# Seven half-block products in place of eight in the third sweep of a symmetric-storage graph kernel

## The reference, cut to what matters

```
h = relu(layernorm(x));  T1 = adj @ h;  T2 = 2 * adj @ T1 - h;  T3 = 2 * adj @ T2 - T1
x = x + (h @ W0 + T1 @ W1 + T2 @ W2 + T3 @ W3 + bias0)
h2 = relu(layernorm(x));  p = tanh(min(|h2|, 10)) * h2 / (|h2| + 1e-8)
s = adj @ p;  y = artanh(min(|s|, 0.999)) * s / (|s| + 1e-8)
x = x + (y @ K + bias1)
```

## Time and profile before

| | |
|---|---|
| median of 3 runs | 1854.3 us |
| the profiled execution | 1854.24 us, span 1852.4 us |
| TensorE busy | 1830.2 us, 99% of the span |
| VectorE, ScalarE, GpSimd busy | 413.7, 121.3 and 41.1 us |
| loads of blocks | 626 of 1 MB, 357 GB/s over the span |
| third sweep | about 1141 us to the end |

### The profile page before, as it was taken

How to read it: one execution, slowest core, us unless ns; L and a number is a source line. 1 busy time by engine, 2 the same in 40 slices (tenths; PEclk the granted TensorE clock), 3 DMA queues, 4 the chain that set the end, 5 groups by cost and what they waited for, 6 DMA issues and landing times.

```text
span 1852.4 us, 22385 instructions
## 1 busy us (share of the span) xinstructions
PE 1830.2 (99%) x9620; PEld 825.3 (45%) x9620; DVE 413.7 (22%) x853; ACT 121.3 (7%) x233; POOL 41.1 (2%) x65
## 2 busy tenths in 40 slices
PE   7999999999999999999999999999999999999997
PEld 4444444444444445444444444344444444444444
DVE  7111111111122123000000001532321222122136
ACT  1000000000000000000000000311000000000014
POOL 0000000000000000000000000000000000000003
PEclk9999999999999999999999999999999999999998
DMA  9999999999999986888888785899999999999995
GB/s 379 421 421 421 421 420 416 387 394 389 399 371 381 374 331 228 319 295 298 295 302 304 263 303 208 331 379 377 372 383 395 384 377 382 407 384 384 406 397 202
DMA packets 94833, 662.31 MB, mean 358 GB/s; under 512 B 11408, under 2 KB 13712, under 8 KB 14608
## 3 DMA queue, kind: packets, MB, share of 16 engines
q1 hardware_dynamic: 93744, 660.64, 91.5%
q10 hardware_dynamic: 992, 0.23, 0.1%
HBM read 658.74 MB, written 2.10 MB: 357 GB/s over the span
## 4 chain that ended last, share of the span: by engine, by line
PE 97%; DVE 1%; DMA 1%; SPq 0%; issue 0%; ACT 0%; DVEq 0%
PE row_bank L523 36%; PE work_bank L503 19%; PE work_bank L537 17%; PE row_bank L492 12%; PE row_bank L525 4%; PE own_bank L553 3%; PE work_bank L505 3%; PE turned L608 2%; DMA ring<-adj_blocks 1%; PE work_bank L577 0%; SPq L417 0%; PE own_bank L564 0%; PE own_bank L608 0%; PE row_bank L608 0%; SPq L428 0%
## 5 line engine op out<-in xcount | busy, mean ns | idle before, releaser
L525 PE MATMUL row_bank<-ring,nodes 128*64 128x512 f32 x1728 | 756.6, 592 | 0.0
L523 PE MATMUL row_bank<-ring,nodes 128*64 128x512 f32 x1728 | 756.6, 592 | 0.0
L523 PEld LDWEIGHTS row_bank<-ring,nodes 128*64 128x64 f32 x1728 | 236.4, 137 | 419.0 <-issue 416.2
L505 PE MATMUL work_bank<-ring,nodes 128*64 128x512 f32 x936 | 420.8, 592 | 0.0
L503 PE MATMUL work_bank<-ring,nodes 128*64 128x512 f32 x936 | 420.8, 592 | 0.0
L537 PE MATMUL work_bank<-ring,nodes 128*64 128x512 f32 x1456 | 342.2, 592 | 0.3 <-DVE nodes L888 0.2
L492 PE MATMUL row_bank<-ring,nodes 128*64 128x512 f32 x1112 | 269.8, 596 | 6.2 <-DMA ring<-adj_blocks 6.2
L525 PEld LDWEIGHTS row_bank<-ring,nodes 128*64 128x64 f32 x1728 | 236.4, 137 | 0.0
L503 PEld LDWEIGHTS work_bank<-ring,nodes 128*64 128x64 f32 x936 | 127.9, 137 | 218.8 <-issue 218.8
L537 PEld LDWEIGHTS work_bank<-ring,nodes 128*64 128x64 f32 x1456 | 124.4, 137 | 169.6 <-issue 167.8
L784 DVE TENSOR_TENSOR partial<-partial,work_bank 128x512 f32<-128x512 f32 x148 | 101.7, 688 | 332.5 <-PE work_bank L537 331.4
(11 more groups left out here) (106 smaller groups left out, 518.4 us busy)
## 6 DMA issues: line engine op xcount, KB each, us to landing
ring<-adj_blocks SPq DMA_DIRECT2D x626, 1024.0 KB, 7.7
out<-resid SPq DMA_DIRECT2D x16, 128.0 KB, 1.9
resid<-x SPq DMA_DIRECT2D x7, 256.0 KB, 11.4
resid<-x SPq DMA_DIRECT2D x2, 128.0 KB, 3.5
w_raw<-cheb_weight ACTq DMA_DIRECT2D x2, 64.0 KB, 7.8
bias<-cheb_bias ACTq DMA_DIRECT2D x1, 32.0 KB, 2.8
bias<-hyp_bias ACTq DMA_DIRECT2D x1, 32.0 KB, 3.8
w_raw<-hyp_kernel ACTq DMA_DIRECT2D x2, 16.0 KB, 8.8
```

What stands on the lines that cost most here:

```text
L505: done = nc.tensor.matmul(bank[EVEN, :], nodes[:, c * C + k, B, :], data[:, k, :], start=k == 0, stop=k == C - 1)
L523: nc.tensor.matmul(bank[ODD, :], nodes[:, c * C + k, A, :], data[:, k, :], start=first and k == 0, stop=last and k == C - 1)
L525: done = nc.tensor.matmul(bank[EVEN, :], nodes[:, c * C + k, B, :], data[:, k, :], start=first and k == 0, stop=last and k == C - 1)
```

## The change

For the `BOTH` visits of rows 6 to 15 in the third sweep (95 visits), a block is cut in four: contraction chunks 0-1 and 2-3, columns 0-255 (`N1`) and 256-511 (`N2`); the 64 features are cut in two halves of 32 (`H`). The product of these 2 by 2 halves is made with seven products in place of eight (the form of Strassen and Winograd). Each product is 2 chunks by 2 levels of 32 features by 256 columns, so a visit is 28 products (56 instructions) in place of 8 products of 64 by 512 (16 instructions). They lie in four column tiles of 32, at partitions 0, 32, 64 and 96. The partial products add up in both row banks, which one row now uses together.

- VectorE makes the three sums of the block's parts, 128 by 1024, 128 by 512 and 128 by 512, into one of two mix slots, in the program two visits ahead of the visit that uses them. TensorE waits for them ahead of its second, fourth and sixth group of products.
- GpSimd makes four sums of the features of a column, 128 by 128 each, after `EXPAND` (`SUMS`), for columns 0 to 13.
- At a row's end ScalarE copies one half bank and exchanges the 32-partition parts of another bank (5 copies), and VectorE makes the row from the four quarters (`JOIN`, six instructions), two visits after the row; its `TURN` is five visits after the row in place of two. The first fast visit of the next row waits until the banks are read.
- Two ring slots become mix slots and four hold the feature sums, so that from row 4 to the last `BOTH` visit the ring of blocks has 7 slots in place of 13.
- `OWN` and level-4 `AGAIN` visits, and `TURN`s of levels 3 and 4, also use 32-column tiles: twice as many products of half the width (16 in place of 8 for a `TURN`).
- `weight_terms()` makes a small mask that is used in `JOIN`.

```diff
+MIX_SLOTS, SUM_SLOTS = (7, 8), (9, 10, 11, 12)
+FAST_FROM = 6
...
+        if level == 3 and row >= FAST_FROM:
+            follow(2 if row < NB - 1 else 1, ("JOIN", row), lambda: None)
+            visits_to_turn = 5
...
+        if last > shared_from:
+            for k in MIX_SLOTS + SUM_SLOTS:
+                slot_free[k] = max(slot_free[k], shared_to)
...
+                if i in mix_no:
+                    n, mixed = mix_no[i], ring[:, MIX_SLOTS[mix_no[i] % 2], :, :]
...
+                    rounds = [(("A11", "B11", 0, high, N1), ("A11", "B11", 1, high, N1)),
+                              (("A12", "B21", 0, low, N1), ("S3", "T3", 0, low, N2)),
+                              (("A12", "B21", 1, low, N1), ("S3", "T3", 1, low, N2)),
+                              (("S4", "B22", 0, low, N2), ("S2", "T2", 0, high, N2)),
+                              (("S4", "B22", 1, low, N2), ("S2", "T2", 1, high, N2)),
+                              (("S1", "T1", 0, high, N2), ("A22", "T4", 0, low, N1)),
+                              (("S1", "T1", 1, high, N2), ("A22", "T4", 1, low, N1))]
+                    for k, pair in enumerate(rounds):
+                        if k in (1, 3, 5):
+                            pe.wait_ge(s_mixed, 3 * n + (k + 1) // 2)
+                        for part, (a, b, h, bank, columns) in enumerate(pair):
+                            for level in (A, B):
+                                lane = level * F + part * H
+                                done = nc.tensor.matmul(bank[lane:lane + H, columns], left(a, h, level), right[b][:, h, :],
+                                                        start=first and k < 2, stop=k == 6, tile_position=(0, lane),
+                                                        skip_group_check=True)
...
-                        for half in (0, 1):
-                            part = slice(half * F, (half + 1) * F)
+                        for lane in range(0, P, size):
+                            part = slice(lane, lane + size)
...
+                for j in mix_before.get(i, []):
+                    n = mix_no[j]
+                    dve.wait_ge(s_visit, visit_no[fast[n - 2]] if n >= 2 else shared_from)
+                    dve.wait_ge(s_landed[slot_of[load_of[j]]], uses_of[load_of[j]] * 16)
+                    nc.vector.tensor_tensor(mixed[:, :, N1].rearrange("p (k h) n -> p k h n", k=2), halves[:, :, :, N2],
+                                            block[:, 0:2, :].rearrange("p h (k n) -> p k h n", k=2), ALU.subtract)\
+                        .then_inc(s_mixed, 1)
+                    dve.wait_ge(s_mixed, 3 * n + 1)
+                    nc.vector.tensor_tensor(mixed[:, 0:2, N2], block[:, 2:4, N2], mixed[:, 0:2, N1], ALU.subtract)\
+                        .then_inc(s_mixed, 1)
+                    dve.wait_ge(s_mixed, 3 * n + 2)
+                    nc.vector.tensor_tensor(mixed[:, 2:4, N2], block[:, 2:4, N1], mixed[:, 0:2, N2], ALU.subtract)\
+                        .then_inc(s_mixed, 1)
```

More of the change, by code:

```diff
@@ L86, in next_is_known @@
         if kind == "AGAIN":
-            return (level[0], col) in known and (level[0] < 4 or ("SUM", row, 3) in steps)
+            summed = ("JOIN", row) if row >= FAST_FROM else ("SUM", row, 3)
+            return (level[0], col) in known and (level[0] < 4 or summed in steps)
         return (2 + sweep[0], col) in known
@@ L159, in work_order, with with_sums @@
         one_visit_passed()
-    return with_batches(steps)
+    return with_batches(with_sums(steps))
+def with_sums(steps):
+    out, waiting, corner = [], [], True
+    for s in steps:
+        out.append(s)
+        if s[0] == "EXPAND" and s[1] < NB - 2:
+            waiting.append(("SUMS", s[1]))
+        if s == ("AGAIN", LOW, LOW, 4):
+            corner = False
+        if not corner:
+            out += waiting
+            waiting.clear()
+    return out
 def is_loaded(kind, row, col, level=0):
@@ L245, in chebyshev_hyperbolic_kernel @@
             turn_no[s[1:]] = turns
+    fast = [i for i, s in enumerate(steps) if s[0] == "BOTH" and phase_of[i] == 2 and s[1] >= FAST_FROM]
+    mix_no = {i: n for n, i in enumerate(fast)}
+    in_order = [i for i, s in enumerate(steps) if s[0] in VISITS]
+    mix_before = {}
+    for i in fast:
+        mix_before.setdefault(in_order[in_order.index(i) - 2], []).append(i)
+    sums_no = {s[1]: n + 1 for n, s in enumerate(s for s in steps if s[0] == "SUMS")}
+    shared_from, shared_to = visit_no[steps.index(("AGAIN", LOW, LOW, 4))], visit_no[fast[-1]]
     slot_free = [0] * SLOTS
     for n, last in enumerate(last_visit_of):
+        if last > shared_from:
+            for k in MIX_SLOTS + SUM_SLOTS:
+                slot_free[k] = max(slot_free[k], shared_to)
         slot = min(range(SLOTS), key=lambda k: slot_free[k])
@@ L316, in chebyshev_hyperbolic_kernel @@
             known_at[s[1], 4] = n
+    fast_rows = [s[1] for s in steps if s[0] == "SUM" and s[2] == 3 and s[1] >= FAST_FROM]
+    for i in fast:
+        assert freed_by[load_of[i]] < visit_no[in_order[in_order.index(i) - 2]]
     norm_at = {s[1]: n + 1 for n, s in enumerate(s for s in steps if s[0] == "NORM")}
@@ L411, in chunks, with features, sum_of @@
             return slice(r * C, (r + 1) * C)
+        H = F // 2
+        N1, N2 = slice(0, BLOCK // 2), slice(BLOCK // 2, BLOCK)
+        def features(c, half, chunk_half):
+            return nodes[:, c * C + 2 * chunk_half:c * C + 2 * chunk_half + 2, :, half * H:(half + 1) * H]
+        feature_sums = ring[:, SUM_SLOTS[0]:SUM_SLOTS[-1] + 1, :, :].rearrange("p s k n -> p (s k) n")
+        def sum_of(c, k):
+            return feature_sums[:, c, k * 4 * H:(k + 1) * 4 * H].rearrange("p (h l f) -> p h l f", h=2, l=2)
         @block.sync
@@ L510, in _ @@
+                if kind == "BOTH" and phase_of[i] > 0 and i not in mix_no:
                     level = phase_of[i] + 1
@@ L534, in _ @@
                     pe.wait_ge(s_landed[slot], landed)
[L535 to L538, removed]
+                    if level < 4:
+                        for k in range(C):
+                            half = (ODD, EVEN)[k % 2]
+                            done = nc.tensor.matmul(bank[half, :], nodes[:, c * C + k, A if level == 3 else B, :],
+                                                    data[:, k, :], start=k < 2, stop=k >= 2)
+                    else:
+                        for k in range(C):
+                            for part in range(2):
+                                lane = k % 2 * F + part * H
+                                done = nc.tensor.matmul(bank[lane:lane + H, :],
+                                                        nodes[:, c * C + k, B, part * H:(part + 1) * H], data[:, k, :],
+                                                        start=k < 2, stop=k >= 2, tile_position=(0, lane))
                     done.then_inc(s_visit, 1)
@@ L551, in _ @@
                     for k in range(C):
-                        half = (ODD, EVEN)[k % 2]
-                        done = nc.tensor.matmul(bank[half, :], nodes[:, c * C + k, A, :], data[:, k, :],
-                                                start=first and k < 2, stop=last and k >= 2)
+                        for part in range(2):
+                            lane = k % 2 * F + part * H
+                            done = nc.tensor.matmul(bank[lane:lane + H, :],
+                                                    nodes[:, c * C + k, A, part * H:(part + 1) * H], data[:, k, :],
+                                                    start=first and k < 2, stop=last and k >= 2, tile_position=(0, lane))
                     done.then_inc(s_visit, 1)
@@ L659, in _ @@
                         .then_inc(s_high, 1)
-                if kind == "SUM" and s[2] == 3 and s[1] > LOW:
+                if kind == "SUM" and s[2] == 3 and s[1] in fast_rows:
+                    r = s[1]
+                    if r > FAST_FROM:
+                        act.wait_ge(s_cleared, fast_rows.index(r))
+                    else:
+                        act.wait_ge(s_visit, visit_no[steps.index(("H_TERM", NB - 1))])
+                    act.wait_ge(s_visit, visit_no[last_of_row["ROW", r, 3]])
+                    nc.scalar.activation(common[:, 1, :], row_banks[1][:, N2], ACT.Copy).then_inc(s_aside, 1)
+                    for lane in range(0, P, F):
+                        for to, come in ((0, H), (H, 0)):
+                            nc.scalar.activation(aside[lane + to:lane + to + H, :], row_banks[1][lane + come:lane + come + H, :],
+                                                 ACT.Copy).then_inc(s_aside, 1)
+                elif kind == "JOIN":
+                    r = s[1]
+                    act.wait_ge(s_joined, fast_rows.index(r) + 1)
+                    nc.scalar.activation(partial[EVEN, r, :], joined[EVEN, :], ACT.Copy).then_inc(s_kept, 1)
+                elif kind == "SUM" and s[2] == 3 and s[1] > LOW:
                     r = s[1]
```

81 lines of the change are left out of this document (76 added, 5 removed).

## The result

The changed kernel takes 1893.1 us (median of 4 runs, 1891.3 to 1896.3) against 1854.2 us before (1853.6 to 1854.9): ratio 1.0212, 95% interval 1.0194 to 1.0229. It is 39 us slower; 1836 was forecast, range 1814 to 1870.

The account below looks back on a forecast made before the run. TensorE was taken as the bound, with DMA 6 to 9% behind. Terms -40.7 + 1 + 7.4 + 0.8 + 4 + 8 + 2 = -17.5, with overlap -18.3, took 1854.3 to 1836 us; range 1814 to 1870.

Parts of the forecast that it names:

- The fast visits: Third sweep, rows 6 to 15: each of 95 `BOTH` visits takes 3.00 us in place of 3.43, -40.7 us.
- rival C: Four tiles don't run abreast, or issue is slower than 28.7 ns: 1900 us to over 2300; chance 0.09.
- The `TURN`s: Levels 3 and 4, 32 instructions for 16: +7.4 us (0 to 7.4) at level 3, +0.8 at level 4.
- Switches of width: Rows 4 and 5, some six changes between 64-wide and 32-wide visits, 0.17 us each: +1 us (0 to 1).
- VectorE's and GpSimd's sums: VectorE's three per block take 1.22, 0.69, 0.69 us, GpSimd's under 3 us per column: +4 us (0 to 20).
- Rival B: VectorE becomes the bound, its sums slowed by DMA and TensorE using the same memory: 1855 us or slower; chance 0.05.
- `JOIN` and the tail: `JOIN` at row ends hidden, also after row 15: 0; loads of columns 14 and 15: +2 us (0 to 6).
- The loads: Rows 7 to 15: 72 alternating pairs need 4.98 us of loading against TensorE's 4.72: +8 us (0 to 18.7).
- The prediction's own sign of being wrong: Wrong if the fast visit isn't 3.00 us, or if idle time in the third sweep is over 35 us.
- Rival A: Short ring makes load latency the bound in alternating pairs, from a landing time of 6.5 us: 1873 us; chance 0.17.

Follow-up runs that it names:

- tiles32: Kernel before with only the change's 32-column tiles for `OWN`, level-4 `AGAIN` and the `TURN`s, `BOTH` staying 64 wide: 1877.3 us, ratio 1.0125.
- mix_other: The change with 7 slots, VectorE making its three sums from features in SBUF without waiting for the block: 1865.6 us, ratio 1.0060.
- nosum: The change with 7 slots, VectorE's sums left out but for the first two fast visits: 1865.1 us, ratio 1.0060.
- half: The change with 7 slots, each load of the third sweep's later part bringing two of four chunks: 1821.9 us, ratio 0.9826.
- ring8: The change with 8 block slots in place of 7, some products using feature sums of wrong columns: 1833.1 us, ratio 0.9885.
- ring9: The change with 9 block slots in place of 7, some products using feature sums of wrong columns: 1826.6 us, ratio 0.9851.

## Why the prediction was wrong, point by point

**The fast visits** were right: 3.02 us for 3.00, -39 of -40.7 us. Four tiles stream abreast, so rival C is out by the rows of the trace.

**The `TURN`s** were mis-sized: +8.2 us forecast, 0 measured. The 28.7 ns of the earlier trace rows was taken for a floor of issue; the same view after shows 14 ns. It was the stream (64 columns, two passes, two abreast: 26.7 ns), which halves with four tiles. The page of the Trainium skill that was weighed there ("TensorE: Matmul & The Clock Gate", Part 2) gives 62 ns per matmul with hardware decode off. The measured 14 ns lies 4 times under it; no run here tells whether decode was on or off.

**Switches of width** (0.17 us each) were nearly right, 0.145 by `tiles32`; the trace of the change has nine of them where some six were reckoned. The Trainium skill says of this ("TensorEngine Tiling (Array Packing)", Key Properties) that changing the tiling mode drains the engine; this case's rows agree, with 0.145 us.

**VectorE's and GpSimd's sums** were right in size (1.24, 0.70, 0.70 for 1.22, 0.69, 0.69) and as a load (`mix_other` and `nosum` are 0.5 us apart; some 6 us in `half`; 4 forecast). Rival B is out.

**`JOIN` and the tail**: between two rows `JOIN` is hidden, as forecast. From a row's last fast visit to the next row's first it is 12.05 us in all nine cases, which is 3.02, five visits of 1.72 and a `TURN` of 0.45. After row 15 it isn't hidden: the fourth `AGAIN` starts 1.68 us late, at 1815.02. The work bank that it needs is added to `partial` behind `JOIN`'s instructions on VectorE, until 1814.91. The tail's loads cost five waits of 0.5 to 1.0 us in the timeline, 3.2 us for a forecast of 2.

**The loads** are the step that failed: +8 us were forecast (0 to 18.7), and the alternating pairs lost 73. The step compared averages, 53.3 with 52.3 us for row 11, and let the ring lose only the difference of two rates, 0.26 us per pair. That is right for a long ring: with nine slots the engines move 413 GB/s and the kernel takes 1827 us, 9 under the forecast. With seven slots the rate falls to 361 to 367 GB/s, and what binds is the loop: a pair takes 5.72 us in the mean, not 4.98. Against TensorE's own 4.74 that is 74 x 0.98 = 73 us. Two fast visits in a row start 3.02 us apart, and the stretches between rows run at TensorE's own speed too, so the account closes: -39 for the streams, +73 for the alternating pairs, +2 before the first fast visit (with the switches) and +6 behind the last make the 42 us between the two spans. The prediction's own sign of being wrong, over 35 us of idle time in the third sweep, was met with 67 us (753 less 686 busy, from 1141 us on; 14 forecast).

Rival A had this mechanism, its formula T = (L + 3.8) / 2 and its point of decision, L = 6.5. I gave it 0.17, because I took today's landing of 7.8 us for a queue that four rotating slots wouldn't build. After the change the median is 7.7 all the same. Put in L = 7.7 and T is 5.75. That this lies so near to 5.72 is partly luck: in the chain the loads take 6.98 and 7.60 us, and the rest of the loop 4.2 in place of 3.8. Single pairs take between 4.7 and 7.9 us; what the slow ones among them wait for wasn't taken apart (they make the mean 0.15 longer than the median, 11 us in all).

Why L stays near 7.7 us is open in part. The queue didn't go away: loads that take 7.7 us each, with one issued every 2.9 us (1.0486 MB at 363 GB/s), are 2.7 under way at a time, and in the trace 136 of the 137 loads issued between 1300 and 1700 us found two or three earlier ones that hadn't landed. L isn't a constant: it is 4.7 us with half the bytes in `half`, and 8.2 and 9.3 with more slots. A fixed lower limit of the DMA engines in this pattern isn't the cause, since the rate goes up to 384, 409 and 413 GB/s in `mix_other`, `ring8` and `ring9`. But why the engines count as busy for 0.96 of the time at 363 GB/s in the change, and for 1.01 at 413 in `ring9`, no run shows.

## What to carry to other kernels

When a change takes buffers from a ring, don't ask only whether the transfers fit on average: write down the loop of one slot (freed, landed, prepared, used), add its parts from the trace with the landing time that it shows under load and not the one of a lone load, and divide by the buffers that really rotate. The landing time moves with the number of loads under way, so the sum is a first estimate, and runs with one or two buffers more test it. Buffers that hold data for later don't rotate: here 7 slots were 4. Anything put between landing and use lengthens the loop, even where the engine that does it has time to spare; and a short ring can be paid with an idle engine's work, as GpSimd's sums, made almost seven times as often, bought three slots and 64 us.

## What the runs showed of the hardware that was not expected

- TensorE started a 64-column float32 instruction of a 32-wide tile, with its weight load, each 14 ns, four tiles abreast (the level-3 `TURN`).
- A change between 64-wide and 32-wide tiles costs 0.145 us (159 changes in `tiles32`, which is 23.4 us slower).
- The time to landing of 1 MB loads hardly tells a short ring from a long one: it is 7.8 with 13 slots before, 7.7 with 7 slots and 7.9 without sums, while the rate goes from 387 to 363 and 380 GB/s. With the fast visits and eight or nine slots it is 8.2 and 9.3 at 409 and 413 GB/s.
- A VectorE sum of two SBUF operands with 1024 elements takes 1.24 us, and 1.34 us with GpSimd busy in over half the time beside it.
